# Three of GpSimd's four transfers per group wait for steps of the other engines, and the weights are loaded beside the constants

## What is computed

```python
x = _layernorm(x + L0(x))   # relu(segment_sum(x[src], dst) @ W.T + b)
x = _layernorm(x + L1(x))   # [x[src'], x[dst'], ea2] @ W1, batch norm over edges, relu, @ W2,
                            #   segment mean over the first index, + x
x = _layernorm(x + L2(x))   # 8-head attention over edges (q, k, v, edge features), skip, norm,
                            #   feed-forward with gelu, norm
x = _layernorm(x + L3(x))   # 4-head additive attention:
# L3: proj = x @ W_proj; s = leaky_relu(src_score[src] + tgt_score[dst])
#     e = exp(s - max(s)); att = e / segment_sum(e, dst)[dst]
#     out = segment_sum(proj[src] * att, dst) + bias
```

## Time and profile before

| | |
|---|---|
| median of 3 runs | 6624.19 us |
| the profiled execution | 6624.27 us |
| its span | 6622.5 us |
| PE busy | 5189.9 us (78%) |
| DVE busy | 4327.9 us (65%) |
| POOL busy | 4019.6 us (61%) |
| ACT busy | 2747.1 us (41%) |
| mean granted TensorE clock | 0.907 of full speed |

### The profile page before, as it was taken

How to read it: one execution, slowest core, us unless ns; L and a number is a source line. 1 busy time by engine, 2 the same in 40 slices (tenths; PEclk the granted TensorE clock), 3 DMA queues, 4 the chain that set the end, 5 groups by cost and what they waited for, 6 DMA issues and landing times. The chain is left out here.

```text
span 6622.5 us, 108943 instructions
## 1 busy us (share of the span) xinstructions
PE 5189.9 (78%) x29030; PEld 3716.2 (56%) x29030; DVE 4327.9 (65%) x15755; ACT 2747.1 (41%) x6645; POOL 4019.6 (61%) x3613
## 2 busy tenths in 40 slices
PE   4777799868886666487868999969898967776798
PEld 3655577744555555433337888735555535555576
DVE  4554677733335555477757888869999955555698
ACT  0000355521111111266643555557777742222355
POOL 4666366666666888677765545315555555544699
PEclk9899899978888788799988999989999978888999
DMA  4555566634445666699974555434444423333476
GB/s 129 169 176 168 155 184 178 172 108 133 131 130 109 106 106 106 117 310 312 302 226 132 149 148 149 116 98 128 131 127 132 127 73 72 74 72 71 127 199 185
DMA packets 1159174, 966.37 MB, mean 146 GB/s; under 512 B 156342, under 2 KB 970882, under 8 KB 1158564
## 3 DMA queue, kind: packets, MB, share of 16 engines
q1 hardware_dynamic: 977956, 684.36, 34.4%
q0 software_dynamic: 158368, 210.14, 15.7%
q10 hardware_dynamic: 22240, 64.90, 2.6%
HBM read 485.30 MB, written 496.79 MB: 148 GB/s over the span
## 5 line engine op out<-in xcount | busy, mean ns | idle before, releaser
L526 POOL DMA_INDIRECT tgt_tab<-l_nodes_ext,rank_at x392 | 452.8, 1155 | 411.4 <-ACT l_nodes_ext L2328 308.6
L1563 POOL DMA_INDIRECT agg<-l_edges_b_rows,l_edges_b_at x392 | 608.6, 1552 | 135.5 <-issue 76.8
L1851 POOL DMA_INDIRECT l_edges_kv<-kv_tab,src_i x392 | 399.6, 1019 | 401.7 <-DVE l_edges_v_e L1872 292.9
L2526 POOL DMA_INDIRECT l_edges_proj<-proj_tab,src_i x392 | 381.8, 974 | 384.0 <-DVE l_edges_msg L2499 254.2
L526 POOL DMA_INDIRECT to_col<-l_nodes_col_s,rank_row x392 | 415.0, 1059 | 323.5 <-ACT l_nodes_col_s L1257 213.8
L968 POOL DMA_INDIRECT l_edges_fetched<-in_x,src_i x392 | 382.6, 976 | 218.9 <-DMA dst_i<-in_dst 111.6
L898 ACT COPY l_edges_rows<-l_edges_sums 128x264 f32<-128x264 f32 (+1 forms) x294 | 122.1, 450 | 944.6 <-DMA dst_i<-in_dst 462.3
L1321 POOL DMA_INDIRECT l_edges_a_at_row<-to_row,src_i x392 | 378.9, 967 | 218.3 <-issue 111.4
L526 POOL DMA_INDIRECT q_tab<-l_nodes_qkvs,rank_at x392 | 401.7, 1025 | 147.4 <-issue 110.7
L851 DVE TENSOR_SCALAR l_edges_hot<-columns,local_edge 128x128 f32<-128x128 f32 (+3 forms) x784 | 257.6, 380 | 295.3 <-DMA dst_i<-in_dst 285.5
L1733 PE MATMUL l_nodes_y<-w_qkvs,l_nodes_x_t 128*128 128x512 f32 x784 | 419.5, 617 | 0.0
(11 more groups left out here) (364 smaller groups left out, 14451.4 us busy)
## 6 DMA issues: line engine op xcount, KB each, us to landing
agg<-zeros ACTq DMA_DIRECT2D x98, 516.0 KB
l_nodes_xg<-x SPq DMA_DIRECT2D x196, 256.0 KB
kv_tab<-l_nodes_qkvs SPq DMA_DIRECT2D x98, 512.0 KB
agg<-l_edges_rows SPq DMA_DIRECT2D x98, 266.0 KB
l_nodes_ag<-agg SPq DMA_DIRECT2D x98, 266.0 KB
proj_tab<-l_nodes_ext SPq DMA_DIRECT2D x98, 264.0 KB
l_nodes_ag<-agg SPq DMA_DIRECT2D x98, 258.0 KB
l_nodes_ag_odd<-agg SPq DMA_DIRECT2D x98, 258.0 KB
```

The costliest lines, as they stand in the source:

```text
L526: pool.indirect_dma_start(table, bass.IndirectOffsetOnAxis(ranks[:, n * G + j:n * G + j + 1].bitcast(U32), 0), rows[:, j, :], None, bounds ...
L1563: pool.indirect_dma_start(agg1[j // 2], bass.IndirectOffsetOnAxis(at[k][:, j:j + 1].bitcast(U32), 0), rows[k][:, j, :], None, compute_op=A ...
L1851: pool.indirect_dma_start(kv[k][:, j, :], None, kv_tab, bass.IndirectOffsetOnAxis(src_i[:, n * G + j:n * G + j + 1].bitcast(U32), 0),).the ...
L2526: pool.indirect_dma_start(proj[k][:, j, :], None, proj_tab, bass.IndirectOffsetOnAxis(src_i[:, n * G + j:n * G + j + 1].bitcast(U32), 0),) ...
```

## The change

Four edits.

1. In `edges_3`, the second, third and fourth gather of a group n (from n = 4 on) wait for `scored` >= n - 2, `tailed` >= n - 1 and `lowered` >= n - 2. With the order of VectorE's round given above, these are steps of the round that follows the one whose `weigh` released the first gather.
2. In `nodes_0`, the second to fourth indirect write of group n wait for `a_copied` >= n + 9, `x_copied` >= n + 3 and `normed` >= 4n + 15 (each held to what the stage reaches). These are steps of ScalarE's round that follows the one with `col` of group n.
3. The 37 transfers of the weights move from `load_weights` into `load_consts`, behind the loads of `dst` and `src` on SyncE's queue. Their semaphores are taken once for the kernel, `attend` and `w0` become buffers of the kernel.
4. The 16 writes of the two masks move from SyncE in `rank_rows` to ScalarE's queue in `gather_sum_edges`, behind two clears and ahead of its rounds. The masks become buffers of the kernel.

```diff
@@ scatter_steps
-            def scatter(pool, i, k, ready, count, rows):
+            def scatter(pool, i, k, ready, count, rows, paces=()):
                 n = place(i, k)
                 pool.wait_ge(ready, count)
                 pool.sem_inc(turn, 1)
                 for j in range(G):
+                    if j and paces:
+                        pool.wait_ge(*paces[j - 1])
                     pool.indirect_dma_start(
...
@@ load_consts
+                        dve.memset(attend[:], 0.0).then_inc(zero_made, 1)
                         dve.memset(zeros[:], 0.0).then_inc(zero_made, 1)
-                        dve.wait_ge(zero_made, 1)
+                        dve.wait_ge(zero_made, 2)
...
                         sp.dma_start(src_i[:], src).then_inc(loaded[1], 16)
+                        begin_weights(sp, zero_made)
...
@@ rank_rows, SyncE
-                        if last_of is not None:
-                            sp.wait_ge(masked, 1)
-                            for table, mask in ((reset_tab, reset_s), (open_tab, open_s)):
-                                for h in range(H2):
-                                    sp.dma_start(table[:, h, :], mask[:]).then_inc(mask_out, 16)
-                            sp.wait_ge(mask_out, 2 * H2 * 16)
                         sp.wait_ge(line_out, 16)
...
@@ gather_sum_edges, ScalarE
+                        for table, mask in ((reset_tab, reset_s), (open_tab, open_s)):
+                            for h in range(H2):
+                                act.dma_start(table[:, h, :], mask[:]).then_inc(cleared, 16)
                         rotation(act, groups, (0, lambda i, k: empty(act, i, k)), (0, clear), loop=False)
-                        act.wait_ge(cleared, 16 * (2 * pairs + 2))
+                        act.wait_ge(cleared, 16 * (2 * pairs + 2 + 2 * H2))
...
+        def begin_weights(sp, cleared):
+            for to, frm in plain:
+                sp.dma_start(to, frm).then_inc(weights_in, 16)
+            with nc.allow_non_contiguous_dma(reason="short columns, once"):
+                for to, name in short:
+                    sp.dma_start(to[:], column(name)).then_inc(weights_in, 16)
+                sp.wait_ge(cleared, 2)
+                for m, name in enumerate(("L3_gnn_a_src", "L3_gnn_a_tgt")):
+                    for h in range(H3):
+                        sp.dma_start(attend[h * C3:(h + 1) * C3, m * H3 + h:m * H3 + h + 1],
+                                     w[name][0, h, :].rearrange("(c a) -> c a", a=1)).then_inc(attend_in, 16)
...
@@ nodes_0, GpSimd
-                        rotation(pool, groups, (0, lambda i, k: scatter(pool, i, k, col_done, place(i, k) + 1, col_s[k])), loop=False)
+                        rotation(pool, groups, (0, lambda i, k: scatter(pool, i, k, col_done, place(i, k) + 1, col_s[k],
+                                                                           ((a_copied, min(place(i, k) + 9, groups)), (x_copied, min(place(i, k) + 3, groups)),
+                                                                            (normed, min(place(i, k) * G + 15, groups * G))))), loop=False)
...
@@ edges_3, GpSimd
                             for j in range(G):
+                                if n >= RING and j:
+                                    pool.wait_ge((scored, tailed, lowered)[j - 1], n - RING + (3 if j == 2 else 2))
                                 pool.indirect_dma_start(
```

More of the change, by code:

```diff
@@ L1020, in gnn, with row, column @@
         bn_scale, bn_shift = sb0("bn_scale", [P, 1]), sb0("bn_shift", [P, 1])
+        w0, attend = sb0("w0", [P, D]), sb0("attend", [P, 2 * H3])
+        def row(name):
+            return w[name].rearrange("(a n) -> a n", a=1).to_broadcast([P, D])
+        def column(name, m=1):
+            return w[name].rearrange("(m p) -> p m", p=P)
+        plain = [(w0[:], w["L0_gnn_W"]), (w1_ab[:, 0:D], w["L1_gnn_W1"][0:D, :]),
+                 (w1_ab[:, D:2 * D], w["L1_gnn_W1"][D:2 * D, :]), (w1_c[:], w["L1_gnn_W1"][2 * D:2 * D + 2, :]),
+                 (w1_2[:], w["L1_gnn_W2"]), (w_e[:], w["L2_gnn_We"]), (w_f1[:], w["L2_gnn_Wf1"]),
+                 (w_f2[:], w["L2_gnn_Wf2"].rearrange("(c p) n -> p c n", p=P)),
+                 (w_proj[:, 0:D], w["L3_gnn_W_proj"]),
+                 (b_0[:], row("L0_gnn_b")), (b_11[:], row("L1_gnn_b1")), (b_12[:], row("L1_gnn_b2")),
+                 (g_2[:], row("L2_gnn_g2")), (b_2[:], row("L2_gnn_b2")),
+                 (b_3[:], row("L3_gnn_bias"))]
+        for m, n in enumerate(("q", "k", "v", "skip")):
+            plain.append((w_qkvs[:, m * D:(m + 1) * D], w[f"L2_gnn_W{n}"]))
+            plain.append((b_qkvs[:, m * D:(m + 1) * D], row(f"L2_gnn_b{n}")))
+        short = [(gamma, "L1_gnn_gamma"), (beta, "L1_gnn_beta"), (g_1, "L2_gnn_g1"), (b_1, "L2_gnn_b1"),
+                   (b_f1, "L2_gnn_bf1"), (b_f2, "L2_gnn_bf2")]
+        total = 16 * (len(plain) + len(short))
+        def begin_weights(sp, cleared):
[9 more added lines that the diff above has]
+                                     w[name][0, h, :].rearrange("(c a) -> c a", a=1)).then_inc(attend_in, 16)
         def split_row(dve, space, row, parts, ready, count, name):
@@ L1065, in load_weights @@
-                for m, n in enumerate(("q", "k", "v", "skip")):
-                    plain.append((w_qkvs[:, m * D:(m + 1) * D], w[f"L2_gnn_W{n}"]))
-                    plain.append((b_qkvs[:, m * D:(m + 1) * D], row(f"L2_gnn_b{n}")))
-                columns = [(gamma, "L1_gnn_gamma"), (beta, "L1_gnn_beta"), (g_1, "L2_gnn_g1"), (b_1, "L2_gnn_b1"),
-                           (b_f1, "L2_gnn_bf1"), (b_f2, "L2_gnn_bf2")]
-                total = 16 * (len(plain) + len(columns))
-                with nc.Block() as block:
-                    @block.sync
-                    def _(sp):
-                        for to, frm in plain:
-                            sp.dma_start(to, frm).then_inc(loaded, 16)
-                        with nc.allow_non_contiguous_dma(reason="short columns, once"):
-                            for to, name in columns:
-                                sp.dma_start(to[:], column(name)).then_inc(loaded, 16)
-                            sp.wait_ge(cleared, 1)
-                            for m, name in enumerate(("L3_gnn_a_src", "L3_gnn_a_tgt")):
-                                for h in range(H3):
-                                    sp.dma_start(attend[h * C3:(h + 1) * C3, m * H3 + h:m * H3 + h + 1],
-                                                 w[name][0, h, :].rearrange("(c a) -> c a", a=1)).then_inc(attend_loaded, 16)
-                        sp.wait_ge(loaded, total)
-                        sp.wait_ge(attend_loaded, 16 * 2 * H3)
```

35 lines of the change are left out of this document (11 added, 24 removed).

## The result

The changed kernel takes 6588.26 us (median of 9 runs, 6581.90 to 6598.96), the kernel before beside it 6614.86 (9 runs): a ratio of 0.9955, 95% interval 0.9945 to 0.9965, or 26.6 us less. On another chip the same kernel gave 0.9959 (0.9940 to 0.9977). The forecast was 6528, 96 us less; the direction and the range held, the size did not. The 26.6 us lie in what the prediction had called "within 33 us", at a chance of 0.20, and 6588 is inside the forecast's own range, 6490 to 6590, by 2 us only, which is luck and says nothing for the 84 us of its Part 1.

The account below looks back on a forecast made before the run. The prediction took TensorE semaphores held behind GpSimd's runs of transfers as the limit in `edges_3`. Setup -12, `edges_3` -84 and `nodes_0` 0 gave -96 from 6624: 6528 us, own range 6490 to 6590, eight in ten 6410 to 6640.

Parts of the forecast that it names:

- within 33 us: Whole kernel: outcome class of a change too small to tell from none, about 0.5%, given chance 0.20.
- Part 1: Added waits in `edges_3`: GpSimd's run ends two gathers earlier, each of 33 holds 2.55 us shorter, 84 us saved.
- What bounds the kernel: No engine fills `edges_3`; TensorE's semaphores are held until GpSimd's run of transfers ends, plus about 1.36 us.
- bound of 190: `edges_3`: most that could be saved with no hold left, cut from 254 for ramps and short holds.
- Same holds, two gathers shorter: `edges_3`: why 84 us was taken between the bounds: one hold in three rounds stays, each 2.55 us less.
- Part 2: Added waits in `nodes_0`: conditions long true, chain of eight writes and its hold stay; 0 us, bounds 91 either way.
- Part 3: Weights loaded beside constants, in the setup: 13.9 us added, 16.2 and 12.1 removed, together -14.4; first edge pass near 52.
- Part 4: Mask writes on ScalarE's queue in `edges_0`: 10.5 us of issues hidden, first copy 2 us late; with Part 3, -12.
- A: Rival: holds nearly vanish in `edges_3`, 190 us saved there, 6422 us in all; chance 0.22.
- C: Rival: holds follow something else or move at the same cost; only the setup's 12 us gained, 6612; chance 0.18.
- D: Rival: a hold in each `nodes_0` round, 91 us more; `edges_3` gains nothing, holds shorter but more frequent; 6703; chance 0.10.
- The warning sign: Whole kernel: prediction is wrong if `edges_3` doesn't shrink or an untouched stage moves by more than 10 us.

Follow-up runs that it names:

- e9b: Changed kernel with GpSimd's gathers of `edges_3` made for the first four groups only (output differs), chip with holds: 6395.18 us, 0.9664 of the kernel before.
- e2: Kernel before with only the three added waits per group in `edges_3`: 6548.29 us, 0.9962 of the kernel before, 25 us less.
- e6b: Changed kernel plus six unused matmuls per group of `edges_3` on TensorE, ahead of its wait for `tailed`, chip with holds: 6495.43 us, 0.9818 of the kernel before.
- e3: Kernel before with only the added waits of the scatter writes in `nodes_0`: 6571.47 us, 0.9999 of the kernel before.
- e1: Changed kernel with the added waits of `edges_3` and `nodes_0` taken out, only the setup edits left: 6567.80 us, 0.9990 of the kernel before.
- e10: Kernel of e5 with three unused matmuls per group of `edges_3` ahead of TensorE's wait for `tailed`: 6575.81 us, 0.9936 of the kernel before.
- e4: Changed kernel with only the third gather's wait for `tailed` kept in `edges_3`, chip without holds: 6030.40 us, 0.9989 of the kernel before.
- e5: Changed kernel, but the second gather of a group in `edges_3` waits for `tailed` too, not `scored`: 6531.71 us, 0.9938 of the kernel before.

## Why the prediction was wrong in size

**What bounds the kernel** was read rightly, for this kind of chip: without gathers the stage runs at the 5.35 us a round that the shortest round showed (5.34), and the kernel is 226.7 us below the one before (e9b), of which 7 are the setup's: 220, between the bound of 190 that I had put on a stage without holds and the 254 that it was cut from. The named releaser, a long landed transfer, was indeed not the real one.

**Part 1 is the step that failed:** "With one such wait in three rounds it is 98 / 3 = 33 times 2.55 = 84 us." The stage gained 33 us in the two profiles, 25 on the whole in e2. Three things stood in the way.
- The count and the size were read off three rounds. The profile of before has not 33 holds of 5.84 us but 26 long ones of 4.70 on the mean; the one studied is among the longest (5.89).
- "Same holds, two gathers shorter" was an assumption about the pattern, not a row. The long holds that remain are shorter than forecast (1.98 us, ending 0.94 after the second gather; I had 3.3 and 1.36), but now 69 of 97 copies are held, by 1.21 us on the mean, where 28 were. The wait for `tailed`, the very step that is held, ties the gathers to the release of the copy, and the next release to the end of those gathers: 0.89 + 0.44 + 4.98 + 0.94 = 7.25 us from copy to copy. The rounds of the 69 take 7.26 on the mean. Before, 41 rounds had neither a hold nor slow products, at 5.38 on the mean; with the pace 5 are left. So seven rounds in ten have a length that faster products don't shorten, and that is why 122 us of long holds became 73 (84 with the short ones) and TensorE's idle time fell by 61 us, not by 84.
- The sum priced TensorE's work at a fixed duration. Its busy time rose by 28 us for the same work: bursts at the full clock fell from 57 to 41 of 95. Not all of the 28 are lost, since 31 of the slow bursts stand in rounds of 7.27 us whose copy is held all the same. They cost in the 23 rounds that aren't held and have products of 4.74 us: 8.09 on the mean against 7.26, some 19 us (an estimate from these rows; no run has this pace with the clock kept up and the holds unmoved).

The profile of before had the clock's part, in the three rounds that the prediction read. The round behind the hold that it studied takes 7.32 us, and the next 5.34; neither is held. TensorE had idled 6.27 us, and its products then took 4.29 and not 2.52:

```profile
6086.50 0.43 PE L509 MATMUL l_edges_tgt_p<-l_edges_parts,l_edges_at_rank 128*128 128x12 bf16 x10 [6.27 <-DVE l_edges_parts L2470]
...
6087.38 4.29 PE L877 MATMUL l_edges_sums<-l_edges_msg,l_edges_hot 128*128 128x132 f32 x20
```

The granted clock, 0.82 in that stage against 0.95 in `nodes_0`, got no term in the sum. e9b (clock 1.00, products 231.4 us for 1839) and e6b (0.97) put the slow bursts at some 95 us of products in the changed kernel.

**Part 2** held: 0.9999 in e3, chains of eight and 5.38 us of wait in the changed kernel. The argument, that the second group's conditions are long true when the chain gets to them, was the right one.

**Part 3** held to a microsecond: the first gather of `edges_0` starts at 52.55 us where it was 66.14, forecast near 52. The weights' issues end at 19.42 and the next block issues at 20.34 (forecast 20.2).

**Part 4** missed its own sign and held on the stage. Sixteen issues took 12.1 us, not 10.5, which was hidden; the first copy comes 18.8 us after the first gather, where it had been 12.8, so 6 us were lost there and not 2. But the stage makes them up: `edges_0` is 648.4 us long against 646.2, and `nodes_0` begins 11.3 us earlier than before. On the three other chips that ran both setups it begins 11 to 16 us earlier. So the -12 held at that point, and e1's 7 us (1 to 12) for the whole kernel mean that some of it may be lost later. That the masks' 3 MB delay the first copy is argued from this; no run took them away.

**The rivals.** A did not occur. C's outcome for `edges_3`, a pace that is worth nothing, is what the second kind of chip shows. D was given 0.10; its holds that come more often while they get shorter, in more than half of the rounds, did occur in `edges_3`, at 69 of 97, and that is most of what ate Part 1. D's price was wrong: the holds are so short that the stage still gains 33 us, and `nodes_0` did not lose its 91. The bound of Part 1 had this pattern too, "8.63 at most", where it is 7.26.

**The warning sign,** an untouched stage that moves by more than 10 us, did come: `nodes_1`. Length and clock of that stage in the changed kernel, in the same kernel again, and in e10, whose `nodes_1` is the same code:

```profile
2766.80:3456.70 689.90, 526.52 (x1568) 244.89 (x1568) 483.12 (x1666) 437.80 (x1078) 489.02 (x441) 0.90 0.88 283
...
2778.90:3461.30 682.40, 520.54 (x1568) 240.48 (x1568) 483.13 (x1666) 436.82 (x1078) 492.47 (x441) 0.92 0.89 286
...
2778.10:3449.50 671.40, 515.57 (x1568) 240.86 (x1568) 483.30 (x1666) 436.75 (x1078) 492.26 (x441) 0.92 0.90 291
```

690, 682 and 671 us for the same instructions: it varies by 17 us on one chip alone (688.2 in e9b, on that of the last two), and one profile of each kernel was too few for a criterion of 10 us. But it can't be put aside either. On each of the four chips that ran both setups, every profile with the new one has a longer `nodes_1` than every profile with the old one: 689.9 against 671.4, 668.8 and 664.1 against 660.8 and 660.0, 660.2 and 654.5 against 649.7, 665.2 and 661.8 against 656.8. That would be 3 to 19 us of the setup's gain; why the setup should reach that stage, no run shows.

**The rules.** Of the Trainium skill I had weighed "SBUF — State Buffer", section "Who interferes with whom", by which TensorE and ScalarE never wait on anyone. That section is on the engines' ports to SBUF. No run here measured a port, so the rule is neither borne out nor refuted, and to read it as a rule on semaphores was my mistake. What the runs show is that semaphores raised by TensorE are seen late in the profiles of three chips, and that on the one where it was tried the time falls by 199.5 us without the gathers (e9b). "DMA: Bandwidth & Descriptors", section "Rules for kernel authors", wants transfers issued early; e2 issued them later and was 25 us faster on the first kind, with nothing lost on the second (e4 with one wait, 0.9989 as e1).

## What to carry over

When a stage's long waits are cut, price what follows them at the clock that the new pattern will be granted: this stage, at .81 after the change, had a second, hidden term (94 us of products beside 166 of idle time), and only a row at either level (2.52 and 4.77 us for one burst) shows its size. Where a change shortens one wait of a self-timed loop over several engines, don't multiply by the old count of waits; let the loop run on in thought for two or three rounds and see when the next one falls. Above all, ask what a new wait closes: here transfers were made to wait for a step that itself waited for the end of the transfers, and the round took the length of that loop, 7.25 us. Count short delays too: with a threshold of 0.6 us two rounds in five look held, with 0.15 it is seven in ten.

The kernel of e6b is the fastest with a right result seen on chips with holds (0.9818), but 1% slower than the kernel before on the others; e5, the setup with the one-gather pace, gave 0.9938 where copies are held, and wasn't run by itself where they are not. Before tuning for a wait like this one, see on which chips it exists.

## What the runs showed of the hardware

The same program takes 6575 to 6622 us on three Trainium2 chips and 6040 to 6042 on three others, 8 to 9% less. Between the changed kernel's profile and that of e4, 555 us apart, 499 lie in `edges_0` (100), `nodes_0` (92), `edges_1a` (94) and `edges_3` with `nodes_3` (213). Of these only `nodes_0` and `edges_3` were read. In `nodes_0` of the changed kernel (first kind) the copies wait 255.8 us, 242.8 of them on no engine in the profile:

```profile
L1259 ACT COPY l_nodes_col_s<-l_nodes_col_p 128x512 f32<-128x512 f32 x97 | 56.9, 587 | 255.8 <-remote 242.8 <-PE l_nodes_col_p L1201 7.9 <-issue 5.1
```

In e4, on the second kind, with the same writes on GpSimd:

```profile
L1259 ACT COPY l_nodes_col_s<-l_nodes_col_p 128x512 f32<-128x512 f32 x94 | 54.9, 584 | 51.6 <-PE l_nodes_col_p L1201 48.3 <-DMA to_col<-l_nodes_col_s,rank_row 3.3
```

`nodes_0` lasts 705.1 us in the changed kernel and 613.6 in e4, from its first instruction to that of the next stage. What sets the two kinds of chip apart, no run shows.
